# A three-level wavelet front on one core: the next tile's gate sums behind the third of four synthesis quads, and two stack clears moved

## The reference

```
cur = img
for _ in range(3):                       # Haar analysis, three levels
    cur, h, v, d = _dwt2(cur);  details.append((h, v, d))
rec = cur * sigmoid(cur.reshape(B, -1) @ Wa + ba)
for (h, v, d), (Wd, bd) in ...:          # synthesis, coarse to fine
    w = softmax(stack([h, v, d]).reshape(B, -1) @ Wd + bd)
    rec = _idwt2(rec, h * w0, v * w1, d * w2)
h = rec
h = h + attention(layernorm(h))          # 16 heads of 16, causal, 256 rows of 256
h = h + experts(layernorm(h))            # router, top 32 rows of each of 16 experts, gated MLP
```

## Time and profile before

| | |
|---|---|
| median of 3 runs | 1186.17 us (1183.14 to 1188.56) |
| profiled execution | 1185.83 us, of which the span is 1184.0 us |
| mean granted TensorE clock | 0.938 |
| TensorE matmuls | 991.5 us, 84% of the span |
| VectorE, ScalarE, GpSimd | 661.5, 590.6, 732.2 us |

### The profile page before, as it was taken

How to read it: one execution, slowest core, us unless ns; L and a number is a source line. 1 busy time by engine, 2 the same in 40 slices (tenths; PEclk the granted TensorE clock), 3 DMA queues, 4 the chain that set the end, 5 groups by cost and what they waited for, 6 DMA issues and landing times.

```text
span 1184.0 us, 19243 instructions
## 1 busy us (share of the span) xinstructions
PE 991.5 (84%) x6998; PEld 825.8 (70%) x6998; DVE 661.5 (56%) x1502; ACT 590.6 (50%) x1105; POOL 732.2 (62%) x658
## 2 busy tenths in 40 slices
PE   0515686988889898887459999999999999999996
PEld 0203355767777777665338888888988888888885
DVE  6768546677777777663635534534544444453441
ACT  0112222777787777786424544544454454454442
POOL 2464233788888878888233765756666665665654
PEclk9967788999999999896669999999999999999999
DMA  8112677797798788711313554454554555554433
GB/s 212 71 71 72 124 138 170 125 131 146 138 140 140 132 151 139 122 36 40 115 54 89 103 107 112 86 108 112 111 103 111 101 95 111 117 99 107 81 54 36
DMA packets 105951, 127.62 MB, mean 108 GB/s; under 512 B 12288, under 2 KB 92160, under 8 KB 104832
## 3 DMA queue, kind: packets, MB, share of 16 engines
q1 hardware_dynamic: 81280, 92.81, 36.5%
q0 software_dynamic: 24576, 33.57, 17.3%
HBM read 79.67 MB, written 46.14 MB: 106 GB/s over the span
## 4 chain that ended last, share of the span: by engine, by line
PE 48%; DVE 2%; POOL 1%; issue 1%; DMA 0%; ACT 0%; POOLq 0%; ACTq 0%
PE y_ps L1170 15%; PE gate_ps L1156 15%; PE value_ps L1156 15%; PE xT_ps L1137 2%; DVE top_index L1310 1%; DVE top L1304 1%; DVE work L1312 0%; PE gate_ps L1179 0%; POOL out L1112 0%; POOL x_rows L1101 0%; DMA x_rows<-normed_scratch,slot_row 0%; DMA rw2s<-in_L_ffn_router_w 0%; ACT xg_hi L1203 0%; DVE L L1302 0%; DVE rw_shifted L1294 0%
## 5 line engine op out<-in xcount | busy, mean ns | idle before, releaser
L1112 POOL DMA_INDIRECT out<-y_rows,slot_row x128 | 202.9, 1585 | 192.3 <-ACT y_rows L1216 163.1
L250 POOL TENSOR_TENSOR probs_k<-probs_full,probs_k 128x512 f16<-128x512 f32 x192 | 223.2, 1170 | 66.1 <-ACT probs_k L652 65.8
L1279 DVE TENSOR_TENSOR hidden<-silu_g,value_ps 128x512 f32<-128x512 f32 x128 | 88.0, 688 | 306.3 <-PE value_ps L1156 171.5
L1224 ACT ACTIVATE silu_g<-gate_ps 128x512 f32<-128x512 f32 x128 | 76.6, 598 | 276.6 <-PE gate_ps L1156 276.6
L1101 POOL DMA_INDIRECT x_rows<-normed_scratch,slot_row x128 | 146.9, 1148 | 56.2 <-issue 38.7
L645 ACT ACTIVATE probs_full<-scoresT_ps,log 128x512 f32<-128x512 f32 x192 | 131.8, 686 | 88.0 <-PE scoresT_ps L476 57.9
L1170 PE MATMUL y_ps<-w_hi,hidden_lo 128*128 128x256 f32 x512 | 144.9, 283 | 0.0
L1170 PE MATMUL y_ps<-w_lo,hidden_hi 128*128 128x256 f32 x512 | 144.9, 283 | 0.0
L1170 PE MATMUL y_ps<-w_hi,hidden_hi 128*128 128x256 f32 x512 | 144.7, 283 | 0.0
L652 ACT ACTIVATE probs_k<-probs_full 128x512 f16<-128x512 f32 x192 | 119.7, 624 | 0.0
L1156 PE MATMUL gate_ps<-xg_hi,w_hi 128*128 128x512 f32 x256 | 103.4, 404 | 2.1 <-ACT xg_hi L1203 2.1
(11 more groups left out here) (206 smaller groups left out, 2335.8 us busy)
## 6 DMA issues: line engine op xcount, KB each, us to landing
w_raw<-in_L_ffn_w SPq DMA_DIRECT2D x48, 512.0 KB, 4.1
q_stack<-q_scratch SPq DMA_DIRECT2D x96, 128.0 KB, 4.9
k_stack<-k_scratch SPq DMA_DIRECT2D x96, 128.0 KB, 8.1
x_tile<-in_x SPq DMA_DIRECT2D x4, 1024.0 KB, 5.2
h_scratch<-rec_tile SPq DMA_DIRECT2D x4, 1024.0 KB, 3.9
hacc<-h_scratch SPq DMA_DIRECT2D x4, 1024.0 KB, 5.4
q_scratch<-q_hi SPq DMA_DIRECT2D x16, 256.0 KB, 2.2
q_scratch<-q_lo SPq DMA_DIRECT2D x16, 256.0 KB, 2.6
```

The lines of the kernel that those rows point to most:

```text
L250: G.tensor_tensor(probs(b, 1, n), pf[N % 3][:].rearrange("p (a q) -> p a q", a=4 if n % 3 == 2 else 2), probs(b, 0, n), ALU.subtract).then ...
L1112: G.indirect_dma_start(out=rows, out_offset=bass.IndirectOffsetOnAxis(ap=idx[:, col:col + 1], axis=0), in_=ys[c][:, j, :], in_offset=None, ...
L1224: A.activation(sg[ft % 2][:], GP[ft % 2][:], ACT.Silu).then_inc(silu_done, 1)
L1279: V.tensor_tensor(hf[ft % 2][:], sg[ft % 2][:], VP[ft % 2][:], ALU.mult).then_inc(hf_done, 1)
```

## The change

On TensorE and ScalarE the gate sums of tile t+1 move from behind the fourth quad of tile t to between its third and fourth. ScalarE's `tile` is cut in two: `gates`, the exponential, goes along, and `diagonals` stays behind the fourth copy. On GpSimd the clear of stack 0 moves ahead of the first split, and the clear of stack 1 into ticks -6 to -2, one piece per tick. `wraw` gets a place of its own among the front's first buffers, and the wait for the weight transposes goes.

```diff
--- before.py
+++ after.py
@@ -112,8 +112,6 @@
         ye = [[sb(f"var_eps{n}_{i}", [P, 2]) for i in range(2)] for n in range(2)]
         yp = [[sb(f"rstd_pow{n}_{i}", [P, 2]) for i in range(2)] for n in range(2)]
         yy = [[sb(f"rstd{n}_{i}", [P, 2]) for i in range(2)] for n in range(2)]
-        with ExitStack() as first:
-            wraw = first.enter_context(nc.sbuf_tensor("wraw", [P, 3, 2, D], F32))
         QS0, KS0, V10 = sb("q_stack0", [P, J, 2, S], F32R), sb("k_stack0", [P, J, S], F32R), sb("v_ones0", [P, 2, H, VW], BF16)
         with ExitStack() as first:
             tb = lambda n, s, d=F32: first.enter_context(nc.sbuf_tensor(n, s, d))
@@ -138,6 +136,7 @@
             ngate = tb("ngate", [P, 10])
             blk = tb("same_image", [P, P])
             tick = tb("tick_split", [P, 1])
+            wraw = tb("wraw", [P, 3, 2, D])
             band, low, Y = [], [], []
             for i in range(2):
                 band.append([tb(f"band{l}_{i}", [P, 3, 8 >> l, D >> l]) for l in (1, 2, 3)])
@@ -260,6 +259,8 @@
 
             def ticks(t0, t1):
                 for t in range(t0, t1):
+                    if -6 <= t < -1:
+                        clear(1, t + 6)
                     if t == 0:
                         g.wait_ge(low_done, 4)
                     if 0 <= t < 5:
@@ -311,16 +312,13 @@
             g.wait_ge(const_done, 4 + IT)
 
             c = Chain(g, split_chain, 0, 0)
+            for k in range(5):
+                clear(0, k)
             tile(1)
             tile(2)
-            g.wait_ge(wt_ps, 3)
-            for k in range(5):
-                clear(0, k)
             g.wait_ge(filled, 3)
             ticks(FIRST, CUT[0])
             tile(3)
-            for k in range(5):
-                clear(1, k)
             ticks(CUT[0], LAST + 1)
 
 
@@ -612,19 +610,19 @@
                     for kt in range(2):
                         ins = pe.transpose(wps[i][:, kt, ft * P:(ft + 1) * P], wraw[:, i, ft, kt * P:(kt + 1) * P], ident[:])
                 ins.then_inc(wt_ps, 1)
+            def synths(t):
+                for k in range(3):
+                    synth(t, k)
+                tile(t + 1)
+                synth(t, 3)
+
             tile(0)
-            for k in range(4):
-                synth(0, k)
-            tile(1)
+            synths(0)
             pe.wait_ge(wt_lo, 3)
             ticks(FIRST, CUT[0])
-            for k in range(4):
-                synth(1, k)
-            tile(2)
+            synths(1)
             ticks(CUT[0], CUT[1])
-            for k in range(4):
-                synth(2, k)
-            tile(3)
+            synths(2)
             pe.wait_ge(rw1_in, 16)
             ticks(CUT[1], LAST + 1)
 
@@ -659,9 +657,11 @@
                 for ft in range(2):
                     A.activation(dst[0][:, ft, :], bank[:, ft, :], ACT.Identity, bias=bqk[:, m, ft:ft + 1]).then_inc(done, 1)
 
-            def tile(t):
+            def gates(t):
                 act.wait_ge(z_ready, t + 1)
                 A.activation(ez[:], z[:], ACT.Exp).then_inc(exp_ready, 1)
+
+            def diagonals(t):
                 act.wait_ge(gate_done, t + 1)
                 for k in range(6):
                     A.activation(diag[:, k], ident[:], ACT.Copy, scale=(gate, ngate)[k // 3][:, 7 + k % 3:8 + k % 3]).then_inc(diag_done, 1)
@@ -728,20 +728,22 @@
             for i, m in enumerate("qkv"):
                 act.wait_ge(wt_ps, i + 1)
                 A.activation(WT[m][0][:], wps[i], ACT.Copy).then_inc(wt_hi, 1)
-            tile(0)
-            for k in range(4):
-                synth_left(0, k)
-            tile(1)
+            def synths_left(t):
+                for k in range(3):
+                    synth_left(t, k)
+                gates(t + 1)
+                synth_left(t, 3)
+                diagonals(t + 1)
+
+            gates(0)
+            diagonals(0)
+            synths_left(0)
             act.wait_ge(c_in, 16 * 3)
             act.wait_ge(filled, 3)
             ticks(FIRST, CUT[0])
-            for k in range(4):
-                synth_left(1, k)
-            tile(2)
+            synths_left(1)
             ticks(CUT[0], CUT[1])
-            for k in range(4):
-                synth_left(2, k)
-            tile(3)
+            synths_left(2)
             ticks(CUT[1], LAST + 1)
```

## The result

The changed kernel takes 1171.43 us (median of 4 runs, 1170.35 to 1173.47), the kernel before 1184.79 (4 runs); the ratio is 0.9885, with a 95% interval of 0.9855 to 0.9914. It is 13.4 us faster; the forecast was 16.5 us faster, 1169.3 us, in a range of 1163 to 1176. (The forecast was counted from 1186.17, the median of three runs; a fourth run of the kernel before, at 1183.41, has lowered it.)

A forecast was written before the change was run, and what follows sets the result against it. The prediction took the chain of splits, layernorms, gates and quads before image 0's first scores at 161.20 as the bound; -5.8 - 5.8 + 0.3 - 3.8 - 1.4 = -16.5 us gave 1169.3 us, range 1163 to 1176.

The forecast's parts named there:

- steps 1 and 2: On GpSimd, the clears of stacks 0 and 1 leave the slots behind tile 2's and 3's splits: 5.8 us gained each.
- The cover named for stack 0's clear: VectorE, splitting tile 0, is held 3.2 us at worst; its later 5.23 us wait for wband covers that.
- step 3: Gate matmul behind the third quad: tile 3's low bands done at 146.9 in place of 150.7, 3.8 us gained.
- the two parts named: At tile 3's gates, VectorE starts 2.9 us earlier, and a slow step of 1.27 us takes 0.4, another 0.9.
- The 0.3 us of delay: The gate matmul on TensorE delays the fourth quad and the next split, twice: 0.3 us lost in all.
- step 4: TensorE's clock stays up in tile 3's first quad after a shorter stop: 1.4 us gained, bounds 0 and 1.4.
- the nearer case: The earlier stop at the same place, before tile 3's first quad, where the clock fell about 3 us later.
- Behind the first scores: From image 0's first scores on, a microsecond won before 161 us is one at the end.
- The clears don't hold VectorE: Rival, 12%: GpSimd's clears hold VectorE's part sums of tile 3 by 2.0 us and the clock falls: 1172.7 us.
- The stall for negmax_lo: Rival, 6%: the gain is given back at the negmax transfers, where the 8.8 us stall grows: about 1183 us.
- The mean granted clock: Rival, 3%: slower, because TensorE's clock in the attention stage drops to a mean near 0.92 in place of 0.938.

The follow-up runs named there:

- e5: The changed kernel with stack 1's five clears put back in one piece behind the split of tile 3: 1175.42 us.
- e1: The changed kernel with the gate sums put back behind the fourth quad, both clears staying moved: 1173.33 us.
- e10: e9 with the gate sums of tiles 1 and 2 behind the fourth quad again, only tile 3's behind the third: 1161.54 us.
- e6: The changed kernel without any edit, profiled a second time: 1168.94 us.
- e7: The changed kernel without any edit, profiled a third time: 1172.01 us.
- e9: The changed kernel with early heads of the splits of tiles 2 and 3, and readerless matmuls ahead of the first quads of tiles 1, 2 and 3: 1161.06 us.

## Why the prediction was right

**Both clears (steps 1 and 2): right in place and size.** 5.78 and 5.77 us against 5.8 each; e5 puts one of them back and finds 5.96 us between tick and var_eps again, e1 has both without the gate edit. The cover named for stack 0's clear held: the wait for wband was 5.69 us. Of stack 1's pieces the third did precede image 2's rstd and nobody waited for it.

**Gate matmul behind the third quad (step 3): right.** 3.78 us against 3.8, from the two parts named (2.84 us earlier behind the sums; a step of 1.27 us at 0.35). The gates of tiles 1 and 2 were hidden, as argued; that this holds only as long as the splits are long, e10 shows. The 0.3 us of delay is the term that was sized wrong. From the third quad to the next split it took 0.23 us longer at tile 0 and 0.93 at tile 1, where the third quad's end met the part sums (TensorE waited 0.43 us for them), because that tile's first quad had been 0.86 us faster. The faster quad and the wait nearly cancel, which is luck: the forecast had neither. Both splits ran 0.12 us longer, which the sum did not have either.

**TensorE's clock (step 4): the term that failed in the profiled execution.** "I take 1.4, since the nearer case is the same place": the clock fell again, the quad took 4.83 us, and the term was 0 there. The gap was as forecast (2.23 us against 2.3). That the stop is what brings the fall is likely and not shown (filled, the clock stayed up in four of four profiles; unfilled, it fell in three of six). What was wrong is to have taken one end for granted. By e6 and e7 the fall is decided execution by execution, at even odds as far as six profiles tell, and the term is worth 1.7 us in the quad step when it comes (5.69 against 7.39), not 1.4: a quad behind such a stop takes 3.14 us at the full clock, and the forecast had set the slow one against 3.43. In e6 it did come, and the scores stood at 144.69 against a forecast of 144.7. Half the term was the value to take; it would have given 1170.0.

**Behind the first scores: right, with 0.8 us on top.** The changed kernel's profile has a granted clock of 0.92 and 0.74 in 170 to 180 us, where the kernel before had 1.0 in the stretch 15 us later; e6 took 41.48 to negmax and e7 42.06. Over all profiles that stretch varies from 38.6 to 42.2, so these 0.8 us are within it. All three profiles of the changed kernel lie above the 41.33 of the one profile before, though, and whether a part of that is the change's own stays open. With the clock term's 1.4 us it makes up nearly all of the 2.3 us by which the profiled execution missed 1169.3.

**The rivals.** The clears don't hold VectorE: stack 0's run beside its splits of tile 0 (1.23 and 1.22 us, as before), and two of stack 1's from 117.95 beside the first of tile 3's part sums, whose steps keep 0.29 us each; the long ones of 2.26 us start at 121.98, behind the two pieces (they end at 119.91). The stall for negmax_lo didn't grow (8.10 us against 8.82). The mean granted clock was 0.939 to 0.947 in the changed kernel's four runs, at or above the 0.938 of before.

## What to carry to other kernels

Look for what an engine does between the event that frees it and the step for which another engine already waits, here two clears of 5.8 us whose stacks were first loaded some 40 us later (q_stack of image 0 at 126.60, of image 1 at 163.56); moving such work cost nothing that these traces show and paid its whole length, as long as the named engine's wait is on the path at that place. When a small step is brought forward, ask which of its repetitions has a consumer that waits: the three gate sums were moved alike and one paid. And after each gain read the same view again: the heads of the splits, which wait for nothing that they use, gave 8.5 us more, and then the part sums were next.

## What the runs showed of the hardware

The granted clock after a stop of 2.2 us is not a property of the kernel: with the same instructions and the same gap, the first quad of tile 3 ran at 2.4 GHz throughout in one profile (granted clock 1.00 over 136 to 138 us) and mostly at 1.2 GHz in two (0.67 and 0.77 there, 0.50 in the two microseconds after). The first quads of tiles 1 and 2, after longer stops, vary likewise: 4.4 to 5.9 us without any edit near them. A term that rests on the clock after a short stop should be taken at its mean, with both ends in the range. Matmuls without a reader, put into the stop, went with a clock that stayed up in four of four profiles. Ahead of the first quads of tiles 1 and 2 in e9 the clock was already at 1.2 GHz. At tile 1 nine of them ran for 4.0 us, TensorE stopped for 0.7, and the clock rose only inside the quad; at tile 2 they stood between the value projection and the transposes without a stop, and it rose before the quad. That the stop made the difference two places don't prove.

VectorE and GpSimd steps can hold each other in both directions. In the kernel before GpSimd's column sum started at 60.93 and took its usual 1.89 us, and VectorE's step at 60.96 was held until it ended. In the changed kernel VectorE was first:

```profile
60.94 0.35 DVE L897 SCALAR_TENSOR_TENSOR col_sum_dif<-band,ngate,low 128x128 f32<-128x128 f32 x1
61.20 1.92 DVE L898 TENSOR_SCALAR v_scaled<-band,gate 128x128 f32<-128x128 f32 x1
```

The column sum, at 60.98 behind the first of these, took 2.06 us, and then held the second, which takes 0.28 us at 133.86 with GpSimd idle, to its end. The same happened at 96.66 to 98.84. That either may be the one that waits, by who starts first, is what the Trainium skill says (page "SBUF — State Buffer", section "Who interferes with whom"). The same section's sentence that a VectorE instruction with two SBUF inputs contends with a GpSimd instruction that reads SBUF, not with one that only writes it, agrees with both places in this trace where a memset ran beside such steps: at 5.76 us (1.23 us, 1.22 before) and from 118.8 us (0.29 us, 0.28 and 0.29 before).
